# First attention of a four-stage block: rows, column strips and V tiles rewritten

## The reference, cut to what matters

```python
kv_in = concat([ctx, x], axis=1)            # 320 keys, 256 columns
q, k, v = x @ q_w + q_b, split(kv_in @ kv_w + kv_b)
attn = einsum('bkhd,bnhd->bhkn', q, k) / 16 # 16 heads of 16 columns
attn = where(mask, attn, -inf)              # mask over the 64 ctx keys
out = einsum('bhkn,bnhd->bkhd', softmax(attn), v) @ out_w + out_b + x
```

## Time and profile before

| what | us |
|---|---|
| median of three runs | 1117.71 |
| the profiled execution's own time | 1119.87 |
| its span, first to last instruction | 1118.1 |
| PE busy (share of the span) | 1031.9 (92%) |
| DVE busy | 664.3 (59%) |
| ACT busy | 458.4 (41%) |
| POOL busy | 340.2 (30%) |

### The profile page before, as it was taken

How to read it: one execution, slowest core, us unless ns; L and a number is a source line. 1 busy time by engine, 2 the same in 40 slices (tenths; PEclk the granted TensorE clock), 3 DMA queues, 4 the chain that set the end, 5 groups by cost and what they waited for, 6 DMA issues and landing times.

```text
span 1118.1 us, 15389 instructions
## 1 busy us (share of the span) xinstructions
PE 1031.9 (92%) x5320; PEld 815.0 (73%) x5320; DVE 664.3 (59%) x1578; ACT 458.4 (41%) x1128; POOL 340.2 (30%) x382
## 2 busy tenths in 40 slices
PE   6999999989998899998979989899998999989898
PEld 4777777778877567775668778688775777757787
DVE  2656565662188885888851255421688858888510
ACT  3555554544245433553333144242454325533331
POOL 2533333442034333443331101011344324433310
PEclk8899999999999999999999999899999999999999
DMA  9000000000034300440000100020244003300000
GB/s 348 4 1 2 1 2 1 2 1 1 1 113 145 130 1 6 132 134 30 1 1 1 36 41 1 1 66 1 77 145 165 1 1 118 128 1 1 1 10 29
DMA packets 14383, 52.43 MB, mean 47 GB/s; under 512 B 1507, under 2 KB 3043, under 8 KB 13028
## 3 DMA queue, kind: packets, MB, share of 16 engines
q1 hardware_dynamic: 14308, 51.46, 13.4%
HBM read 50.40 MB, written 1.05 MB: 46 GB/s over the span
## 4 chain that ended last, share of the span: by engine, by line
PE 77%; DMA 8%; DVE 8%; ACT 3%; issue 2%; POOL 1%; SPq 0%; DVEq 0%; ACTq 0%
PE ps L962 10%; PE ps L786 10%; PE ps L810 9%; PE ps L949 9%; DMA ring<-in_heads_dram 8%; PE ps L624 5%; PE ps L603 4%; PE ps L709 4%; PE ps L711 3%; PE ps L750 3%; PE ps L570 3%; PE ps L739 3%; PE ps L798 2%; PE ps L621 2%; PE ps L557 2%
## 5 line engine op out<-in xcount | busy, mean ns | idle before, releaser
L786 PE MATMUL ps<-arena,hT 128*128 128x512 f32 x256 | 119.3, 610 | 14.6 <-ACT hT L1111 14.6
L440 POOL TENSOR_TENSOR arena<-arena,rinv 128x640 f32<-128x640 f32 x64 | 80.2, 1252 | 147.6 <-DVE rinv L1320 147.6
L810 PE MATMUL ps<-arena,pT 128*128 128x256 f32 x512 | 116.5, 381 | 7.5 <-ACT pT L1188 4.7
L949 PE MATMUL ps<-hT,w 128*128 128x256 f32 x512 | 118.2, 388 | 4.8 <-ACT hT L1130 4.8
L1420 DVE TENSOR_TENSOR x<-ps,x 128x512 f32<-128x512 f32 x16 | 11.1, 692 | 187.3 <-PE ps L962 187.3
L962 PE MATMUL ps<-w,arena 128*128 128x256 f32 x512 | 113.3, 380 | 1.8 <-DVE x L1420 1.8
L949 PEld LDWEIGHTS ps<-hT,w 128*128 128x128 f32 x512 | 98.6, 195 | 19.1 <-issue 5.8
L449 POOL TENSOR_TENSOR rstd<-var,neg_half 128x1 f32<-128x1 f32 (+1 forms) x56 | 36.5, 651 | 247.7 <-DVE var L1351 247.7
L810 PEld LDWEIGHTS ps<-arena,pT 128*128 128x128 f32 x512 | 94.8, 190 | 21.4 <-ACT pT L1188 5.6
L962 PEld LDWEIGHTS ps<-w,arena 128*128 128x128 f32 x512 | 97.2, 190 | 15.5 <-issue 2.5
L1141 ACT ACTIVATE arena<-ps,cols 128x256 f32<-128x256 f32 x128 | 53.6, 470 | 111.2 <-PE ps L949 111.2
(11 more groups left out here) (152 smaller groups left out, 2092.6 us busy)
## 6 DMA issues: line engine op xcount, KB each, us to landing
ring<-in_heads_dram SPq DMA_DIRECT2D x64, 512.0 KB, 3.5
w<-in_w_dram SPq DMA_DIRECT2D x8, 1024.0 KB, 8.1
x<-in_x_dram SPq DMA_DIRECT2D x1, 1024.0 KB, 11.0
lnb<-in_lnb_dram SPq DMA_DIRECT2D x4, 256.0 KB, 8.6
ring<-in_wp_dram SPq DMA_DIRECT2D x1, 1024.0 KB, 4.7
out_dram<-x SPq DMA_DIRECT2D x4, 256.0 KB, 2.1
arena<-in_kinT_dram SPq DMA_DIRECT2D x1, 960.0 KB, 8.6
brow<-in_brow_dram SPq DMA_DIRECT2D x1, 768.0 KB, 12.3
```

Of the source, the lines that this page charges most:

```text
L440: g.tensor_tensor(w, w, rinv[:, n % 2, 0:2].unsqueeze(2).broadcast_to([P, 2, KEYS0]), ALU.mult)\
L786: last = mm(ps[:, half, :], hT[:, k, d, 0:P], A[:, d, b // 2, cols_of, sl, :].rearrange("p r s k -> p r (s k)"), start=(d == 0), stop=(d = ...
L810: last = mm(ps[:, 6, 0:D], pT[:, k, c, :], VW[:, b, c, :], start=(c == 0), stop=(c == PAIRS - 1))
L949: last = mm(ps[:, f // 2, (f % 2) * 256:(f % 2 + 1) * 256], w1[:, d, f * P:(f + 1) * P], hT[:, k, d, :], start=(d == 0), stop=(d == 1))
```

## The change

- Spread: `copies` becomes four full 128 x 128 matrices, one for each 32-row strip, with zeros in the other rows; spread reads all 128 rows of `HL`. The scale -1/16 moves into the matrix for Q, so the maximum becomes a minimum and line 1305 is gone. The mask matmul is float32r on 128 rows.
- Scores: Q of the two heads lies in two tiles of `Q0` with zeros in the other head's half, K in `K0`; each head is one matmul of 320 columns on 128 rows. ACT moves K and head 0's Q, DVE head 1's Q (`kq_dve`).
- Order: four steps form a quad of two pairs (`step0`). Values runs in every second iteration for two steps, of two neighbouring pairs, matmul by matmul in turn; the two write different 32-partition strips of bank 6. `turn` and `copy0` come one iteration later, `values` two; `prob0` and `pT0` have four buffers.
- V: five tiles of 128 keys per batch in key order (`values_of`), all moved by ACT. `ctxD` is not needed in L0 any more and is loaded behind `brow`. ACT reads the values of eight steps at once.
- Inserts: two `base` in one even iteration (banks 7 and 6), V and `output` in even iterations.

Runs of more than two removed lines are left out here, since the kernel before stands above. Of PE:

```diff
+        JOBS = [("kc", m) for m in range(4)] + [("vc", b) for b in range(B)]
...
+        def step0(n):
+            quad, s = n // 4, n % 4
+            return quad // 4, 2 * (quad % 4) + s % 2, s // 2
+        def last_step0(pair):
+            return 4 * (pair // 2) + 2 + pair % 2
...
             def attend0():
                 N = TILES * PAIRS
-                def pair_of(n):
-                    return n // 2, n // 2 // PAIRS, (n // 2) % PAIRS, n % 2
...
                 def base(t):
...
+                    o = ps[:, 6, 256:512] if w else ps[:, 7, 0:KEYS0]
...
+                        last = mm(o, w0[:, w, d, m * P:(m + 1) * P], kinT[:, d, b, C * w:KEYS0],
...
+                def values_of(b, j):
+                    o = v0_out(b, j)
+                    if j < 2:
+                        for v in range(2):
+                            for d in range(DH):
+                                at = C * j + v * P
+                                last = mm(o[:, v * P:(v + 1) * P], kinT[:, d, b, at:at + P], vw0[:, d, :, j, :],
+                                          start=(d == 0), stop=(d == 1))
+                    else:
+                        for d in range(DH):
+                            mm(o[0:C, 0:P], kinT[:, d, b, S:KEYS0], vw0[:, d, :, 0, :], start=(d == 0), stop=(d == 1))
+                            last = mm(o[C:P, 0:P], kinT[:, d, b, 0:C], vw0[:, d, :, 1, :], start=(d == 0), stop=(d == 1))
+                    last.then_inc(v0_ps, 1)
...
-                    m, at = r // 4, slice(32 * (r % 4), 32 * (r % 4) + 32)
+                    m, j = r // 4, r % 4
...
-                        last = mm(ps[:, 7, 0:width], copies[at, w, c, :], HL[at, m, c, cols_of],
+                        last = mm(ps[:, 7, 0:width], copies[:, j, w, c, :], HL[:, m, c, cols_of],
...
-                        last = mm(ps[:, 7, 0:C], e48[one, :], mask[one, 0, b * C:(b + 1) * C], start=False, stop=True)
+                        last = mm(ps[:, 7, 0:C], e48[:, :], mask0[:, b * C:(b + 1) * C], start=False, stop=True)
...
                     pe.wait_ge(kq_ready, 2 * pair + 2)
+                    pe.wait_ge(kq_dve, pair + 1)
...
+                        last = mm(ps[:, 2 * (n % 2) + e, 0:KEYS0], Q0[:, pair % 3, e, u * P:(u + 1) * P],
+                                  K0[:, pair % 3, :], start=True, stop=True)
...
-                                                   prob0[:, n % 3, c * P:(c + 1) * P], ident[:, :])
+                                                   prob0[:, n % 4, c * P:(c + 1) * P], ident[:, :])
...
-                    pe.wait_ge(pt0_ready, n + 1)
...
-                    if pair >= 4:
-                        pe.wait_ge(o0_ready, pair - 3)
...
+                    pe.wait_ge(pt0_ready, n + 2)
+                    if n % 8 == 0 and n > 0:
+                        pe.wait_ge(o0_ready, n // 8)
+                    for c in range(VT0):
+                        for i in (n, n + 1):
+                            b, r, u = step0(i)
+                            at = slice(32 * (r % 4), 32 * (r % 4) + 32)
+                            last = mm(ps[at, 6, u * P:(u + 1) * P], V0[:, b, c, r, :], pT0[:, i % 4, c, :],
+                                      start=(c == 0), stop=(c == VT0 - 1))
...
+                    bank = 7 if g == TILES - 1 else 6
...
                 base(1)
-                project(1, 2)
-                pe.wait_ge(base_copied, 2)
+                pe.wait_ge(in_vw0, 16)
+                values_of(0, 0)
+                values_of(0, 1)
...
-                for i in range(N + 3):
+                for i in range(N + 4):
+                    step, b = i % 16, i // 16
                     if i < N:
                         scores(i)
                     if i + 4 < N:
...
+                        if i == 1:
+                            pe.wait_ge(base_copied, 3)
+                        elif step in (9, 13) and b + 1 < B:
+                            pe.wait_ge(base_copied, 4 * (b + 1) + (1 if step == 9 else 3))
                         spread(i + 4)
...
+                    if 3 <= i < N + 3:
+                        turn(i - 3)
+                    if i >= 5 and i % 2 == 1:
...
+                        values(i - 5)
...
+                    if i == 0 or step in (8, 12) and b + 1 < B:
                         if i == 8:
                             pe.wait_ge(in_kin, 16)
                         pe.wait_ge(kq_ready, i + 5)
...
+                        base(2 if i == 0 else 4 * (b + 1) + (0 if step == 8 else 2))
+                    if step == 0 and b < B:
+                        if b == 0:
+                            pe.wait_ge(base_copied, 2)
+                        values_of(b, 2)
+                    elif i == 2:
+                        pe.wait_ge(v0_ready, 3)
+                        base(3)
+                    elif step in (4, 6) and 1 <= b < B:
+                        output(2 * (b - 1) + (0 if step == 4 else 1))
+                    elif step in (8, 12) and b + 1 < B:
+                        if step == 12:
+                            pe.wait_ge(o0_ready, 2 * b + 1)
+                        base(4 * (b + 1) + (1 if step == 8 else 3))
+                    elif step in (10, 14) and b + 1 < B:
+                        values_of(b + 1, 0 if step == 10 else 1)
...
-                    pe.wait_ge(rows_done, g)
```

Of ACT:

```diff
+            def values_of0(b, j):
+                act.wait_ge(v0_ps, 3 * b + j + 1)
+                o = v0_out(b, j)
+                if j < 2:
+                    last = a_(V0[:, b, 3 * j:3 * j + 2, :, HD * j:HD * j + HD],
+                              o.rearrange("p (t r c) -> p t r c", t=2, r=PAIRS), ACT.Copy)
+                else:
+                    a_(V0[0:C, b, 2, :, 0:HD], o[0:C, 0:P].rearrange("p (r c) -> p r c", r=PAIRS), ACT.Copy)
+                    last = a_(V0[C:P, b, 2, :, HD:2 * HD], o[C:P, 0:P].rearrange("p (r c) -> p r c", r=PAIRS), ACT.Copy)
+                last.then_inc(v0_ready, 1)
...
-                width = S if w else KEYS0
                 act.wait_ge(kq_ps, n + 1)
                 if pair >= 3:
...
+                    act.wait_ge(s0_ps, last_step0(pair - 3) + 1)
+                if w == 0:
+                    a_(K0[:, pair % 3, :], ps[:, 7, 0:KEYS0], ACT.Copy).then_inc(kq_ready, 1)
+                else:
+                    a_(Q0[0:C, pair % 3, 0, :], ps[0:C, 7, 0:S], ACT.Identity, bias=col("row48")[0:C, :])\
+                        .then_inc(kq_ready, 1)
...
-                    last = a_(prob0[:, n % 3, e * KEYS0:(e + 1) * KEYS0], ps[:, j, 0:KEYS0], ACT.Exp,
-                              bias=nb[:, n % 2, 1, e:e + 1], scale=1.0 / HD, accum_out=sm[:, n % 2, e:e + 1])
+                    last = a_(prob0[:, n % 4, e * KEYS0:(e + 1) * KEYS0], ps[:, 2 * (n % 2) + e, 0:KEYS0], ACT.Exp,
+                              bias=nb[:, n % 2, e:e + 1], scale=-1.0, accum_out=sm[:, n % 2, e:e + 1])
...
+            def values0(half):
+                b, d = half // 2, half % 2
+                act.wait_ge(pv0_ps, 4 * (half + 1))
+                if b >= 2 and d == 0:
                     act.wait_ge(o_ps, 2 * (b - 1))
...
+                a_(oT0[:, b % 2, :, d, :], ps[:, 6, 0:2 * P].rearrange("p (u n) -> p u n", u=2), ACT.Identity,
+                   bias=col("L0_v_b", d)).then_inc(o0_ready, 1)
...
-                if i >= 4 and i % 2 == 0:
-                    values0((i - 4) // 2)
...
+                if i >= 11 and i % 8 == 3:
+                    values0(i // 8 - 1)
```

Of DVE, and of the arrays:

```diff
-            v.tensor_copy(copies[:, :, :, :], copies_f).then_inc(copies_ready, 1)
+            for j in range(4):
+                last = v.tensor_scalar(copies[:, j, :, :, :], copies_f, col("strip", j), None, ALU.mult)
+            last.then_inc(copies_ready, 1)
...
+            link(v.tensor_copy(mask_f[:, :], mask_i[:, :]))
+            v.tensor_scalar(mask0[:, :], mask_f[:, :], 0.0, -MASKED, ALU.is_equal, ALU.mult)
+            link(v.tensor_copy(mask2[:, :], mask_u[:, :]))
+            v.tensor_scalar(mask2[:, :], mask2[:, :], 0.0, MASKED, ALU.is_equal, ALU.mult)
+            dve.wait_ge(consts_ready, 1)
+            for e in range(2):
+                far = slice(C * (1 - e), C * (1 - e) + C)
+                v.tensor_scalar(Q0[far, :, e, :], ones[far, 0:1].unsqueeze(2).broadcast_to([C, 3, S]), 0.0, None, ALU.mult)
+            v.tensor_copy(e48[:, :], e48_f[:, :]).then_inc(mask_ready, 1)
...
+            def spread0(n):
+                pair = n // 2
+                dve.wait_ge(kq_ps, n + 1)
+                if pair >= 3:
+                    dve.wait_ge(s0_ps, last_step0(pair - 3) + 1)
+                v.tensor_scalar(Q0[C:P, pair % 3, 1, :], ps[C:P, 7, 0:S], col("row48")[C:P, :], None, ALU.add)\
+                    .then_inc(kq_dve, 1)
...
-                link(v.tensor_reduce(nb[:, n % 2, 0, :], ps[:, j:j + 2, 0:KEYS0], AX.X, ALU.max))
-                v.tensor_scalar(nb[:, n % 2, 1, :], nb[:, n % 2, 0, :], -1.0 / HD, None, ALU.mult).then_inc(nb_ready, 1)
```

(48 more changed lines are left out.)

247 lines of the change are left out of this document (86 added, 161 removed).

## The result

The changed kernel took 1066.52 us (median of four runs, 1061.86 to 1071.92) beside 1117.58 (1114.6 to 1119.65) of the kernel before: ratio 0.9536, 95% interval 0.9502 to 0.957. Run again with the experiments it took 1071.18 beside 1117.41: 0.9539 (0.9465 to 0.9613). The profiled execution took 1061.86, its span is 1060.1. The forecast was 1062.

What follows compares the result with a forecast made beforehand. PE's own list was taken to bound L0. Savings of 46.6 in batches, 6 at the start and 2.3 + 1.2 at the end made 56, from 1119.87 to 1063.9, so median 1062; range 1048 to 1080, with rivals 1046 to 1091.

Steps and rivals of the forecast that it cites:

- Two column strips side by side: Values in L0: the two strips' streams run at once, 1.07 us for two steps, with 2.14 as the other end.
- The two rivals against it: Values: strips take turns, 1090 us, chance 25%; or each change of strip also drains the array, 1132 us, chance 4%.
- the rule: Trainium skill: a weight load overlaps a running matmul only where the row group differs, so strips would take turns.
- The loop of a pair: L0, two steps: scores, maximum, inversion, copy, transposes, values and change back close at 4.35 us, against 5.57 before.
- PE has time to spare in the pair: L0, two steps: PE's work is 3.65 of 4.35 us, and it waits 0.69 before the odd transposes.
- The inserts: Base, split, V tiles and outputs in L0: 7.0 us a batch where 12.7 stood, bounds 4.0 and 12.7.
- Start: L0 up to the first insert: scores(0) at 19.0 instead of 20.61, eight cheaper steps; 6 us saved (3 to 9).
- End: L0 from 221.6 us on: 2.3 saved up to the last scores, 1.2 in all from there through the last outputs.
- The rivals on the inserts and on the clock: Inserts stay at 12.7 a batch or DVE is slower, 1080 us, 10%; clock falls, 50 us or more slower, 1%.
- the third rival: Strips overlap, but inserts keep 12.7 a batch (+17) or the loop is 4.9 (+18); 1080 us, chance 10%.
- The forecast's own range: Whole kernel: 1048 to 1080 us around 1062, by bounds on inserts, start, mask and scores; chance 60%.
- The sum: L0: 46.6 saved in three batches, 6 at the start, 2.3 and 1.2 at the end, together 56 us.

Runs made afterwards that it cites:

- the first experiment: Changed kernel with all five value matmuls of step n, then all five of n+1, instead of alternating: 1090.27 us, ratio to the kernel before 0.976.

## Why the prediction was right

**Two column strips side by side: right.** Twenty value instructions take 1.22, forecast 1.07 + 0.13. The two rivals against it fell: by the prediction's own figures strips that take turns would have shown 2.14 + 0.13, and a drain at each change of strip 1.35 more. Nor is the rule borne out here that the prediction quoted against it, by which weight loads would keep two strips on the same rows apart: the measurement decides. The prediction did not say, and the first experiment shows, that the gain needs the two strips alternating; one after the other they take 1.89.

**The loop of a pair: right, part by part.** Scores to maximum 0.59 (forecast 0.59), maximum and inversion 0.94 (0.98), copy to the odd transposes 0.95 (0.88), these 0.67 (0.70), values with the change back 1.22 (1.20): 4.37 against 4.35.

**PE has time to spare in the pair: wrong at the even step.** Ahead of the odd transposes the room is there: the row's 0.49 counts from PE's last result, and by distances of starts, as the prediction counts, it is 0.65 against 0.69 (76.03 to 76.92 less the 0.24 that this spread takes where nothing waits). But at the even step PE's path and DVE's tie at the copy. The prediction lost nothing by it, since the spread on 128 rows took that path's work off; that is in part luck. The experiment with 32 rows showed it, 12.7 us where 0.2 a pair, 6 us, had been expected. DVE's work was given as 4.1, but the terms written for it add up to 3.91; measured it is 3.92 (75.03 to 78.95), with head 1's Q at 0.49 instead of 0.42.

**The inserts: the term mis-sized.** A batch was to be eight pairs of 4.35 and 7.0 for inserts, 41.8; it is 43.8, so 8.8 for inserts. Base, split and the V groups take 4.18 instead of 2.9 at each of two places: the values start at 86.76, 92.60 and 99.68, and 5.84 + 7.08 less two pairs of 4.37 is 4.18. The outputs cost 0.36 (two pairs of 4.55) instead of 1.0. What failed is the price of the split, taken from the earlier trace rows at 0.33 and 0.49, where it ran ahead of POOL's product: beside it cast and subtraction take 0.96 and 1.39. Moving them gave 3.2 a batch back, more than the whole miss of 2.0. So three batches saved 40.7 where 46.6 was forecast.

**Start: 6 saved by forecast, 4.0 in the first two profiles, 5.3 by the means of two each.** The first spread (13.86, forecast 14.8) and the first scores (18.18, forecast 19.0, before 20.61) come early enough, 2.4 saved up to there; the eight steps behind them add 1.6 in these profiles. From 26 to 34 us it is DVE's list that holds them: DVE is busy 7.37 of the 8 us (in both profiles) and PE 3.71, where in the kernel before PE was busy for all 8 and DVE for 4.88. Two splits stand there beside POOL, a cast of 1.06 and a subtraction of 1.35 among them. Moving the splits took 1.7 off the start (first insert at 43.24, mean 44.95 without). From 34 to 38 us the granted clock is 0.50 and 0.57, in the two profiles of the kernel before 0.76 and 0.63; what that costs was not tested.

**End: the step that the prediction had wrong.** 2.3 + 1.2 saved by forecast, 1.1 measured. Up to the last scores it is 2.8 (176.90 to 189.44, against 15.3 before). From there to `output(6)` 7.5 was forecast for one step's own chain, 8.56 before; it is 10.58, timeline of PE:

```profile
189.44 0.54 PE L591 MATMUL ps<-K,Q 128*128 128x320 f32 x2
190.94 0.73 PE L602 MATMUL ps<-ident,arena 128*128 128x128 f32 x5 [0.96 <-DVE pT_all L1313]
...
192.82 0.77 PE L602 MATMUL ps<-ident,arena 128*128 128x128 f32 x5
194.60 0.74 PE L602 MATMUL ps<-ident,arena 128*128 128x128 f32 x5 [1.01 <-DVE pT_all L1313]
...
196.48 0.76 PE L602 MATMUL ps<-ident,arena 128*128 128x128 f32 x5
198.16 1.29 PE L615 MATMUL ps<-pT_all,arena 128*32 128x128 f32 x20 [0.92 <-DVE pT_all L1313]
```

Since `turn` comes one iteration later, four of them (steps 60 to 63) and three values still stand behind the last scores, and each `turn` needs the banks that the copy of the one before it empties. So the last `turn` starts 7.0 after the last scores. Behind `output(6)` 0.3 is gained. The second profile has 10.58 too.

**The rivals on the inserts and on the clock.** The inserts did become dearer than the forecast's 7.0 a batch, but not as dear as the 12.7 of the third rival. The granted clock stays 1.00 from 50 to 204 us, so nothing of the gain in the batches went to it. The forecast's own range was given as 1048 to 1080; the bounds named for it add up to 1047 to 1085, which changes nothing here.

**The sum.** 56 was forecast for L0 and 47 measured: 5.9 less in the batches, 2.4 at the end, 0.7 at the start. The median 1066.5 stands only 4.5 above 1062 because the later stages came out to its side in the first comparison, and that is luck; with the run beside the experiments (1071.18 beside 1117.41) the gain is 46.2, which is L0's 47. Both times lie in the range, and the sign and the mechanism are the forecast's; a sixth of the forecast gain did not come.

**Where the 47 come from.** By taking parts back one at a time: the interleaved strips 17, the spread on all rows 12.7 (the mask left as changed), the scores on all rows 2.2. Some 15 are left for the values' change of shape once in two steps instead of in each, the step's instructions gone from DVE, the V tiles and the start; these were not separated, and parts taken back one at a time need not add up.

## What to carry to other kernels

Write out the order of each engine's own list, find the loop that runs through both, and look for a second path that ties with it before calling an engine's time spare: the list gave the pair within 0.02 us here, and the tie was missed. Do the same for the last steps of a loop, where the pipeline runs empty: one step's own chain is not what ends last if earlier steps share its buffers. When an edit moves work on DVE, look at what GpSimd does at the new place, and whether the instruction ahead of it is what starts GpSimd. When a new order brings two users of one PSUM bank closer together, look for the wait of the second. Where later stages vary by more than the edit is worth, compare at a point inside the profile that repeats, as the first matmul of the next stage does here.

## What the hardware showed that was not expected

- Two column strips overlap only so far as the order of instructions puts them close: 20 instructions in 1.22 us alternating, in 1.89 one strip after the other, where the second ran only some 0.4 us of work ahead.
- DVE's cast of 128x320 took 0.96 beside GpSimd's product and 0.32 without it, its subtraction of two SBUF tiles of 128x256 1.39 and 0.42; both ended 0.2 to 0.3 after the product, as if they had stood still for it. Moving both ahead of what starts the product took 3.2 us off a batch of 43.8.
- Taking the scores from 128 to 64 rows gained nothing: 0.04 or 0.05 off the distance from scores to spread, 0.09 on that from spread to mask.
- The same later stages took 856.0 to 872.1 us from profile to profile, more than most of these edits are worth. Between two profiles of one kernel 9.6 of 10.9 us were PE's busy time with the same instructions, with a granted clock of 0.80 against 0.93 in one stretch.
